# First x tiles of part two loaded and normalised earlier, and the row of ones of the stacked keys written by DMA

## The chip, the cores and the metric

The kernel runs on one core of a Trainium2 chip. The metric is the device time of one execution in microseconds; the median of three runs is given with the lowest and the highest.

## The reference

The input x is (8, 2048, 256) in float32. The reference is one transformer-like layer of two parts, each with a residual around it and layer norms without weights:

```python
x = x + layernorm(attn(layernorm(x)))
x = x + layernorm(ffn(layernorm(x)))
```

The attention is a Nystrom attention with 16 heads of size 16 and 64 landmarks, each the mean of 32 tokens:

```python
k, q, v = split_heads(x @ Wk), split_heads(x @ Wq) / 4, split_heads(x @ Wv)
q_l, k_l = means of q and of k over 32 tokens           # 64 landmarks per head
s1 = softmax(q @ k_l.T)                                 # 2048 x 64
s2 = softmax(q_l @ k_l.T)                               # 64 x 64
s3 = softmax(q_l @ k.T)                                 # 64 x 2048
out = (s1 @ (pinv(s2) @ (s3 @ v))) @ Wo + bo            # pinv: six Newton-like iterations
```

The second part mixes each token with the one before it (`xr = x_prev + mu_r * (x - x_prev)`, `xk` likewise) and computes `sigmoid(xr @ W_r.T) * (relu(xk @ W_k.T)**2 @ W_v.T)`.

## The kernel before, in words

The eight rows of the batch (2048 tokens each) go through two parts. Each engine has one program written in order; semaphores say what it waits for.

**Part one** takes the rows in two groups of four. For each row it loads x whole (`x1in`), computes mean and variance of every token (`mv1`, `rstd1`, kept for part two), pools the landmarks, projects them, stores queries and keys of the landmarks to DRAM (`lm_dram`, SyncE, line 460), and inverts s2 by six iterations of matrix products. The last inverse leaves VectorE as X (line 1028), and ScalarE's queue stores it to DRAM (`zt_dram`, line 728, semaphore `zt_out`).

**Part two** takes row by row (b) in chunks (c) of 512 tokens. Its tiles lie in the memory that part one used. The order of its stages is written out by hand: PRO once, then BODY seven times, then LAST. Every engine walks through this one list and does its share of each stage (`part2_program`). The stages at the start are: X (SyncE loads a chunk of x into `xin`, two buffers), XA (VectorE makes the normalised `xhat` of it, four instructions of 256 columns, line 1046), R (TensorE transposes xhat into the two `bank`s, ScalarE and VectorE split it into two float16 halves `xT`), AQ, AK and AV (projections), Q and K (SyncE loads the landmarks' block-diagonal tiles `q_bd` and `kA_bd`, eight transfers each), KC (SyncE stacks the halves of k into `k_stack`, twelve transfers), B1 and B2 (row maxima over q_bd and k, matmuls of line 1381, maxima of line 1086), C1 and C2 (token maxima). FS, the scores of s3, comes after all chunks of the row.

`k_stack` has 97 partitions in use: three blocks of 32 with the high and low halves of k, and in partition 96 a row of ones (KS - 1), against which `q_stack` holds the negative maxima. The ones never change; FS waits for them once.

At the joint of the parts every engine waits until part one is over. VectorE, ScalarE, SyncE and GpSimd wait for all steps and for the inverses in DRAM (`zt_out`); TensorE waits for all steps of VectorE and ScalarE, and then, in stage R, for the first xhat. Then GpSimd clears six tiles (lines 604 to 609) and writes the row of ones with four memsets on one partition (line 616), SyncE issues the first two loads of x, and VectorE makes xhat of both.

Of the kernel before, what the change touches and what calls it, by code (L numbers as in the profile page):

```python
# [15 lines left out]
def sandwich(nc, x, Wk, Wq, Wv, Wo, bo, W_r, W_k, W_v, mu_r, mu_k, out):  # L16
# [23 lines left out]
    with ctx:  # L40
        def sb(name, shape, dt=F32, c=ctx):
            return c.enter_context(nc.sbuf_tensor(name, shape, dt))

        def sem(name):
            return ctx.enter_context(nc.semaphore(name))
# [16 lines left out]
        sel4 = sb("sel4", [P, 2 * KB])  # L62
        eye = sb("eye", [P, M])
        ident16 = sb("ident16", [P, P], F16)
        eye7 = sb("eye7", [P, M], F16)
        eye15 = sb("eye15", [P, M], F16)
        eye13 = sb("eye13", [P, M], F16)
# [130 lines left out]
        def of(steps, i, *key):  # L198

            return place[id(steps)][(i, *key)]  # L200
# [53 lines left out]
        class Norm:  # L254
# [40 lines left out]
            def apply(self, dve, dst, src, g, c):  # L295
# [13 lines left out]
        bd_cleared = sem("bd_cleared")  # L309
        stack_cleared = sem("stack_cleared")  # L310
        ones_set = sem("ones_set")
        KS = 3 * 32 + 1
        x_in = [sem(f"x_in{i}") for i in range(2)]
        bank_full = [sem(f"bank{i}_full") for i in range(2)]
# [35 lines left out]

        PRO = [("X", 0), ("XA", 0), ("X", 1), ("XA", 1), ("R", 0), ("X", 2), ("X", 3), ("Q", 0), ("AK", 0), ("XA", 2),
# [79 lines left out]
        def _(sp):  # L433
            def load_rows(i, rows):
                for s in rows:
# [4 lines left out]
                    sp.dma_start(x1in[s % NX1][:, :, :], x[bass.ds(n, 1)].rearrange("a (t p) n -> p (a t) n", p=P))\  # L440
                        .then_inc(p_in[s], 16)

            load_rows(0, [0])
            for w, (dst, src) in enumerate([(wq, Wq), (wk, Wk), (wv, Wv), (wo, Wo)]):
                sp.dma_start(dst[:, :, :], src.rearrange("(k p) n -> p k n", p=P)).then_inc(weights_in, 16)
# [8 lines left out]
            for i in range(B // GR):  # L454
                load_rows(i, range(0 if i else 1, GR))
                for s in ROWS:
                    n = i * GR + s
                    sp.wait_ge(p_dve, of(dve_steps, i, "lmlo", s))
                    hold(sp)
                    sp.dma_start(lm_dram[bass.ds(n, 1)].rearrange("a p n -> p (a n)"),  # L460
                                 lm16[s][:, :, :, :].rearrange("p a k m -> p (a k m)")).then_inc(lm_out, 16)
            sp.wait_ge(lm_out, 16 * B)
            sp.wait_ge(zt_out, 16 * B)

            sp.wait_ge(p_pe, len(pe_steps))
            sp.wait_ge(p_dve, len(dve_steps))
            sp.wait_ge(p_act, len(act_steps))

            def load_q_stack(b):

# [17 lines left out]
            def stage_X(at, b, c):  # L488
                if b > 0 or c >= 2:

                    sp.wait_ge(x_applied, b * NC + c - 1)
                src = x[bass.ds(b, 1), c * CH:(c + 1) * CH, :].rearrange("a (t p) n -> p (a t) n", p=P)
                sp.dma_start(xin[c % 2][:, :, :], src).then_inc(x_in[c % 2], 16)

            def stage_Q(at, b, c):

# [65 lines left out]
        def _(pool):  # L562
# [28 lines left out]
            pool.wait_ge(const_made, 5)  # L591
            g.tensor_tensor(eye[:, :], ident[:, 0:M], ident[:, M:P], ALU.add).then_inc(const_made, 1)

            pool.wait_ge(eyes_made, 4)
            for s in ROWS:
                for t in (XT_bd, ST_bd, ZT_bd):
# [13 lines left out]
            pool.wait_ge(bd_cleared, 2)  # L610
            pool.wait_ge(stack_cleared, 1)
            pool.wait_ge(setup2, 3)
            for c in range(NC):
                if c:
                    pool.wait_ge(ones_set, c)
                g.memset(k_stack[KS - 1:KS, :, c * CH:(c + 1) * CH], 1.0).then_inc(ones_set, 1)

            def stage_OA(at, b, c):
                n = b * NC + c
# [247 lines left out]
        def _(dve):  # L867
# [162 lines left out]
                    ahead(it, 3)  # L1030


            dve.wait_ge(p_act, len(act_steps))
            dve.wait_ge(p_pe, len(pe_steps))
            dve.wait_ge(lm_out, 16 * B)
            dve.wait_ge(zt_out, 16 * B)

            def stage_XA(at, b, c):
                if b or c >= 2:

                    u = (at["R", c - 2] if c >= 2 else at["R", c + 2, 1]).bank
                    for k in range(KB):
                        dve.wait_ge(bank_full[k], u + 1)
                dve.wait_ge(x_in[c % 2], 16 * (b * 2 + c // 2 + 1))
                for t in range(NT):
                    ins = v.tensor_scalar(xhat[c % 2][:, t, :], xin[c % 2][:, t, :], mv1[b][:, c * NT + t, 0:1],
                                          rstd1[b][:, c * NT + t:c * NT + t + 1], ALU.subtract, ALU.mult)
                ins.then_inc(x_applied, 1)

            def stage_R(at, b, c):  # L1050

# [158 lines left out]
        def _(pe):  # L1210
# [209 lines left out]
            def stage_FS(at, b, i):  # L1420
                u = at["FS", i]
                if i == 0:

                    for k in range(KB):
                        pe.wait_ge(bank_drained[k], at["M", 0].bank + 1)
                    pe.wait_ge(q_stack_in, 16 * 3 * HB * (b + 1))
                    pe.wait_ge(k_stack_in, 16 * NKS * NC * (b + 1))
                    pe.wait_ge(ones_set, NC)
                    pe.wait_ge(setup2, 3)
                for w in range(2):  # L1430
                    t = 2 * i + w
                    pe.wait_ge(wide_drained[w], u.wide)
                    for a in range(PAIRS):
                        ins = mm(wide[w][:, a * P:(a + 1) * P], k_stack[0:KS, a, t * P:(t + 1) * P],  # L1434
                                 q_stack[0:KS, a, :], start=True, stop=True)
                    ins.then_inc(wide_full[w], 1)
# [195 lines left out]
```

## Time and profile before

| what | value |
|---|---|
| median of 3 runs | 1943.8 us |
| lowest, highest | 1938.8, 1947.53 us |
| the profiled execution | 1952.56 us |
| its span | 1950.8 us |
| TensorE, matmuls busy | 1590.1 us (82%) |
| VectorE busy | 1439.3 us (74%) |
| ScalarE busy | 984.0 us (50%) |
| GpSimd busy | 254.0 us (13%) |
| granted TensorE clock, mean | 0.918 |

All times of rows are microseconds from the start of the span of the profiled execution, which takes 1.8 us more in all. PE is TensorE, DVE VectorE, ACT ScalarE, POOL GpSimd, SP SyncE; a q behind a name (SPq, ACTq) is that engine's sequencer, here issuing DMAs. "L1046" is a line of the kernel. A row of a timeline merges equal instructions that follow one another. The clock is the share of full speed that TensorE was granted, 1.0 being 2.4 GHz and 0.50 being 1.2 GHz.

### The profile page before, as it was taken

The numbers are of one execution on the slowest core, as the hardware profiler recorded it, in microseconds if no ns is written. First come the engines' busy times: TensorE is split into PE (matmuls) and PEld (weight loads), VectorE is DVE, ScalarE is ACT, GpSimd is POOL, SyncE is SP. The second block draws the span as 40 slices with busy tenths as digits, with TensorE's granted clock in tenths as the row PEclk, the third lists the DMA queues.
The fourth block names the chain that finished last, engine by engine and source line by source line (L and its number), as shares of the span: only waits on it lengthen the run. The fifth ranks groups of instructions, "written<-read, shape, count | busy, mean of one in ns | idle before, by whom it ended". The sixth has DMA issues, their size and how long they took to land. (4 is left out here: it accounts for less than half of the span.)

```text
span 1950.8 us, 50437 instructions
## 1 busy us (share of the span) xinstructions
PE 1590.1 (82%) x21132; PEld 1094.9 (56%) x21132; DVE 1439.3 (74%) x3164; ACT 984.0 (50%) x1599; POOL 254.0 (13%) x134
## 2 busy tenths in 40 slices
PE   2677865786568989989988998998899899888786
PEld 1567755776335557556555744655564465556454
DVE  6889859777763796688579668957966895795465
ACT  1277714774224646545554654456465445645542
POOL 4000000001200111112011101211110121120112
PEclk9789986989778999999999999999999999999888
DMA  6400020001221212112131212213121121311110
GB/s 213 141 3 3 3 74 4 3 3 46 56 58 30 66 51 70 51 50 77 32 87 52 70 50 51 75 33 87 51 69 50 51 77 33 87 41 46 34 33 33
DMA packets 125697, 104.60 MB, mean 54 GB/s; under 512 B 30368, under 2 KB 123424, under 8 KB 125472
## 3 DMA queue, kind: packets, MB, share of 16 engines
q1 hardware_dynamic: 124320, 99.29, 18.2%
q8 instruction: 168, 2.75, 0.6%
q10 hardware_dynamic: 1152, 2.10, 0.3%
q14 instruction: 57, 0.47, 0.1%
HBM read 56.23 MB, written 19.92 MB: 39 GB/s over the span
## 5 line engine op out<-in xcount | busy, mean ns | idle before, releaser
L797 ACT ACTIVATE p<-wide 128x1024 f32<-128x1024 f32 x128 | 124.0, 1021 | 123.5 <-PE wide L1517 122.8
L1094 DVE TENSOR_REDUCE m<-wide 128x16 f16<-128x1024 f32 x128 | 150.4, 1216 | 41.8 <-PE wide L1401 41.5
L1577 PE MATMUL bank<-wrT,xrT 128*128 128x256 f32 x512 | 142.5, 440 | 46.1 <-ACT vv L763 36.1
L774 ACT ACTIVATE e<-wide 128x1024 f32<-128x1024 f32 x128 | 124.4, 1021 | 81.7 <-PE wide L1434 70.4
L1577 PEld LDWEIGHTS bank<-wrT,xrT 128*128 128x128 f32 x512 | 111.6, 223 | 72.0 <-issue 40.0
L1086 DVE TENSOR_REDUCE m<-wide 128x2 f32<-128x1024 f32 x128 | 149.8, 1212 | 2.9 <-PE wide L1381 2.9
L641 POOL TENSOR_TENSOR ob<-ob,xm 128x1024 f32<-128x1024 f32 x32 | 77.0, 2405 | 475.1 <-DVE ob L299 475.1
L1557 PE MATMUL bank<-wo,oT 128*128 128x256 f32 x512 | 120.9, 390 | 6.2 <-DVE xT L1054 3.6
L1587 PE MATMUL acc<-xkT,wkT 128*128 128x512 f32 x256 | 120.1, 613 | 7.1 <-DVE xkT L1167 7.1
L1599 PE MATMUL bank<-wvT,ka 128*128 128x256 f32 x512 | 117.6, 383 | 1.3 <-ACT x2T L822 0.8
L625 POOL TENSOR_TENSOR xm<-yy,xres 128x1024 f32<-128x1024 f32 x32 | 76.1, 2378 | 326.1 <-issue 265.7
L635 POOL TENSOR_TENSOR xkT<-x2T 128x1024 f32<-128x1024 f32 x32 | 60.6, 1893 | 433.2 <-ACT x2T L822 433.2
L1557 PEld LDWEIGHTS bank<-wo,oT 128*128 128x128 f32 x512 | 96.4, 193 | 25.7 <-issue 8.2
L1599 PEld LDWEIGHTS bank<-wvT,ka 128*128 128x128 f32 x512 | 95.3, 190 | 16.2 <-issue 1.9
L1130 DVE TENSOR_TENSOR oT<-acc,oT 128x512 f32<-128x512 f32 x64 | 42.1, 681 | 78.9 <-ACT oT L808 78.9
L1453 PE MATMUL acc<-e,vv 128*17 128x64 f32 x4096 | 77.6, 224 | 25.0 <-ACT e L774 21.0
L1343 PE MATMUL bank<-xT,w 128*128 128x512 f16 x384 | 92.0, 391 | 3.8 <-ACT x2T L822 1.9
L1343 PE MATMUL acc<-xT,w 128*128 128x512 f16 x384 | 93.3, 395 | 1.5 <-DVE xT L1054 1.5
L830 ACT ACTIVATE sg<-bank 128x512 f32<-128x512 f32 x64 | 38.1, 597 | 108.9 <-PE bank L1577 89.4
L1365 PE MATMUL bank<-w,xT 128*128 128x256 f16 x768 | 89.2, 273 | 3.8 <-ACT x2T L822 2.8
L975 DVE COPY ST_bd<-ST_d 64x1024 f16<-64x1024 f16 x192 | 81.0, 422 | 11.5 <-DVE ST_d L966 0.5
L1453 PEld LDWEIGHTS acc<-e,vv 128*17 128x17 f32 x4096 | 62.0, 99 | 42.8 <-issue 28.6
(283 smaller groups left out, 3766.9 us busy)
## 6 DMA issues: line engine op xcount, KB each, us to landing
x1in<-in_L_attn_x SPq DMA_DIRECT2D x8, 2048.0 KB, 10.0
xin<-in_L_attn_x SPq DMA_DIRECT2D x32, 512.0 KB, 4.1
k_stack<-kh SPq DMA_DIRECT2D x256, 64.0 KB, 2.0
xres<-in_L_attn_x SPq DMA_DIRECT2D x32, 512.0 KB, 4.1
out<-ob SPq DMA_DIRECT2D x32, 512.0 KB, 5.3
k_stack<-kl SPq DMA_DIRECT2D x128, 64.0 KB, 2.0
q_stack<-landmarks SPq DMA_DIRECT2D x192, 4.0 KB, 1.6
inverse<-X ACTq DMA_DIRECT2D x8, 256.0 KB, 2.2
```

The costliest lines, as they stand in the source:

```text
L774: sc.activation(e3[w][:, :], wide[w][:, :], ACT.Exp).then_inc(wide_drained[w], 1)
L797: sc.activation(p1[:, 2 * j:2 * j + 2, :], wide[w][:, :].rearrange("p (a n) -> p a n", a=2), ACT.Exp).then_inc(wide_drained[w], 1)
L975: ins = v.tensor_copy(dst[r, :, :, j * M:(j + 1) * M], src[r, :, :, :])
L1086: v.tensor_reduce(m3[:, 2 * j:2 * j + 2, c], wide[j % 2][:, :].rearrange("p (a n) -> p a n", a=2), AX.X, ALU.max).then_inc(wide_drained[j ...
L1094: v.tensor_reduce(m1[:, tiles, 2 * w:2 * w + 2, :].rearrange("p t q x -> p q t x"), wide[w][:, :].rearrange("p (q t x m) -> p q t x m", q= ...
L1343: ins = mm(dst[o][:, :], w16[:, w, wt, k, o * P:(o + 1) * P], xT[:, xt, k, :], start=(i == 0), stop=(i == len(TERMS) - 1))
L1365: ins = mm(bank[j][:, t * A:(t + 1) * A], xT[:, xt, k, tok], w16[:, 2, wt, k, :], start=(i == 0), stop=(i == len(TERMS) - 1))
L1453: ins = mm(acc[k][32 * q:32 * q + HS + 1, j * M:(j + 1) * M], vv[:, 2 * i + w, h, :], e3[w][:, h * M:(h + 1) * M], start=(w == 0 and j == ...
L1557: ins = mm(dst, oT[:, k, tok], wo[:, k, :], start=(k == 0), stop=(k == KB - 1))
L1577: ins = mm(bank[j][:, t * A:(t + 1) * A], xrT[:, k, tok], wrT[:, k, :], start=(k == 0), stop=(k == KB - 1))
L1587: ins = mm(acc[o][:, :], wkT[:, k, o * P:(o + 1) * P], xkT[:, k, :], start=(k == 0), stop=(k == KB - 1))
L1599: ins = mm(bank[j][:, t * A:(t + 1) * A], ka[:, k, tok], wvT[:, k, :], start=(k == 0), stop=(k == KB - 1))
```

## The change

Four things are done.

- SyncE issues the first two loads of x (row 0, chunks 0 and 1) right after the last landmark store of part one, behind three conditions: all rows are pooled, the last landmark projections are done, and the weights are split (`w16_lo`). These are what still reads the memory in which `xin` and `xhat` lie.
- VectorE does stage XA of the two chunks behind the last X of part one and ahead of its waits for the end of part one.
- GpSimd no longer writes the row of ones. At the start of the program it fills a tile `ones16` (128 x 128, float16), and at the joint SyncE copies it into partition 96 of `k_stack` by one DMA (32 KB), ahead of the other transfers of part two.
- The four entries X and XA of chunks 0 and 1 go from the head of PRO.

The core of the diff:

```diff
+        ones16 = sb("ones16", [P, P], F16)
...
-        PRO = [("X", 0), ("XA", 0), ("X", 1), ("XA", 1), ("R", 0), ("X", 2), ("X", 3), ("Q", 0), ("AK", 0), ("XA", 2),
+        PRO = [("R", 0), ("X", 2), ("X", 3), ("Q", 0), ("AK", 0), ("XA", 2),
...
+            def load_x(b, c):
+
+                src = x[bass.ds(b, 1), c * CH:(c + 1) * CH, :].rearrange("a (t p) n -> p (a t) n", p=P)
+                sp.dma_start(xin[c % 2][:, :, :], src).then_inc(x_in[c % 2], 16)
...
+            sp.wait_ge(p_pooled, B)
+            sp.wait_ge(p_pe, of(pe_steps, B // GR - 1, "qk", GR - 1))
+            sp.wait_ge(w16_lo, 3)
+            hold(sp)
+            load_x(0, 0)
+            load_x(0, 1)
             sp.wait_ge(lm_out, 16 * B)
             sp.wait_ge(zt_out, 16 * B)
...
+            sp.wait_ge(ones_made, 1)
+            sp.dma_start(k_stack[KS - 1:KS, :, :], ones16[:, :]).then_inc(ones_set, 16)
...
+            g.memset(ones16[:, :], 1.0).then_inc(ones_made, 1)
             pool.wait_ge(eyes_made, 4)
...
-            for c in range(NC):
-                if c:
-                    pool.wait_ge(ones_set, c)
-                g.memset(k_stack[KS - 1:KS, :, c * CH:(c + 1) * CH], 1.0).then_inc(ones_set, 1)
...
-            dve.wait_ge(p_act, len(act_steps))
-            dve.wait_ge(p_pe, len(pe_steps))
-            dve.wait_ge(lm_out, 16 * B)
-            dve.wait_ge(zt_out, 16 * B)
-
             def stage_XA(at, b, c):
...
+            for c in range(2):
+                stage_XA(None, 0, c)
+
+            dve.wait_ge(p_act, len(act_steps))
+            dve.wait_ge(p_pe, len(pe_steps))
+            dve.wait_ge(lm_out, 16 * B)
+            dve.wait_ge(zt_out, 16 * B)
...
-                    pe.wait_ge(ones_set, NC)
+                    pe.wait_ge(ones_set, 16)
```

VectorE's program at the joint, before (X is the last step of part one, xhat is stage XA, xT stage R):

```order
700 L1028 TENSOR_SCALAR X<-acc 128x512 [waits p_pe]
701 L1198 MEMSET x2T 128x2 [waits zt_out,lm_out,late_in,p_pe,p_act]
702 L1046 TENSOR_SCALAR xhat<-xin,mv,rstd 128x256 [waits x_in0]
703 L1046 TENSOR_SCALAR xhat<-xin,mv,rstd 128x256 x3
704 L1046 TENSOR_SCALAR xhat<-xin,mv,rstd 128x256 [waits x_in1]
705 L1046 TENSOR_SCALAR xhat<-xin,mv,rstd 128x256 x3
706 L1054 TENSOR_TENSOR xT<-bank,xT 128x512 [waits x_hi] x2
```

The same place after the change:

```order
700 L1040 TENSOR_SCALAR X<-acc 128x512 [waits p_pe]
701 L1053 TENSOR_SCALAR xhat<-xin,mv,rstd 128x256 [waits x_in0]
702 L1053 TENSOR_SCALAR xhat<-xin,mv,rstd 128x256 x3
703 L1053 TENSOR_SCALAR xhat<-xin,mv,rstd 128x256 [waits x_in1]
704 L1053 TENSOR_SCALAR xhat<-xin,mv,rstd 128x256 x3
705 L1213 MEMSET x2T 128x2 [waits zt_out,lm_out,late_in,p_pe,p_act]
706 L1069 TENSOR_TENSOR xT<-bank,xT 128x512 [waits x_hi] x2
```

The eight xhat instructions stand ahead of the memset that carries the waits for `zt_out`, where they stood behind it.

SyncE's queue from the last landmark stores to the loads of `q_bd`, before:

```order
15 L460 DMA landmarks<-lm 128x512 [waits p_dve] x4
16 L493 DMA xin<-in_L_attn_x 128x4x256 [waits p_dve,p_pe,p_act,zt_out,lm_out]
17 L493 DMA xin<-in_L_attn_x 128x4x256
18 L493 DMA xin<-in_L_attn_x 128x4x256 [waits x_applied] x2
19 L486 DMA q_bd<-landmarks 16x2x64 [waits bd_cleared]
```

And after the change:

```order
15 L467 DMA landmarks<-lm 128x512 [waits p_dve] x4
16 L448 DMA xin<-in_L_attn_x 128x4x256 [waits w16_lo,p_pooled,p_pe]
17 L448 DMA xin<-in_L_attn_x 128x4x256
18 L483 DMA k_stack<-ones 1x128x128 [waits p_dve,p_act,p_pe,ones_made,zt_out,lm_out]
19 L448 DMA xin<-in_L_attn_x 128x4x256 [waits x_applied] x2
20 L502 DMA q_bd<-landmarks 16x2x64 [waits bd_cleared]
```

The first two loads have left the wait for `zt_out` behind them, and the copy of the ones stands now behind that wait, ahead of chunks 2 and 3 and of `q_bd`.

## Rows read from the trace of the kernel before

**Rows 1.** Windows: stretch, length, busy (and count) per engine, clock, DMA, GB/s.
```profile
478.14:499.73 21.59, 0.00 (x0) 0.03 (x1) 15.21 (x10) 0.00 (x0) 16.76 (x10) 0.58 0.28 97
499.73:1950.80 1451.07, 1265.23 (x13200) 800.60 (x13200) 1044.38 (x2260) 728.79 (x1200) 213.59 (x96) 0.94 0.21 56
```

**Rows 2.** Timeline of TensorE: start, duration, instructions, idle time before and its releaser.
```profile
477.27 0.87 PE L1243 MATMUL acc<-ZT_d,ST_bd 128*128 128x64 f16 x24 [0.81 <-DVE ST_bd L975]
499.73 1.94 PE L1336 MATMUL bank<-ident,xhat 128*128 128x128 f32 x8 [21.59 <-DVE xhat L1046]
503.13 5.28 PE L1343 MATMUL acc<-xT,w 128*128 128x512 f16 x12 [1.46 <-DVE xT L1054]
...
511.21 0.40 PE L1381 MATMUL wide<-kh,q_bd 32*128 32x512 f16 x4
...
519.97 2.75 PE L1343 MATMUL acc<-xT,w 128*128 128x512 f16 x12
...
578.75 0.61 PE L1434 MATMUL wide<-q_stack,k_stack 97*128 97x128 f16 x8 [1.80 <-DVE m L1094]
```

**Rows 3.** Timeline of VectorE at the joint; rows may overlap, taken from several windows.
```profile
479.04 0.68 DVE L1028 TENSOR_SCALAR X<-acc 128x512 f32<-128x512 f32 x1
...
486.17 13.31 DVE L1046 TENSOR_SCALAR xhat<-xin,mv,rstd 128x256 f32<-128x256 f32 x4 [3.74 <-DMA xin<-in_L_attn_x]
...
488.60 7.28 DVE L1046 TENSOR_SCALAR xhat<-xin,mv,rstd 128x256 f32<-128x256 f32 x2
...
499.40 1.36 DVE L1046 TENSOR_SCALAR xhat<-xin,mv,rstd 128x256 f32<-128x256 f32 x4
501.57 1.46 DVE L1054 TENSOR_TENSOR xT<-bank,xT 128x512 f16<-128x512 f32 x2 [0.81 <-ACT xT L742]
```

**Rows 4.** Timeline of GpSimd at the joint; the last row is part of the one above.
```profile
482.25 0.31 POOL L604 MEMSET q_bd<- 128x256 f16 x1 [456.94 <-DMA inverse<-X]
...
484.57 0.31 POOL L609 MEMSET wbd<- 128x256 f32 x1
485.02 14.30 POOL L616 MEMSET k_stack<- 1x4096 f16 x4
...
488.59 7.14 POOL L616 MEMSET k_stack<- 1x4096 f16 x2
```

**Rows 5.** Timeline of SyncE's queue at the joint.
```profile
482.18 18.98 SPq L493 DMA_DIRECT2D xin<-in_L_attn_x  x4
501.20 3.77 SPq L486 DMA_DIRECT2D q_bd<-landmarks  x8
```

**Rows 6.** Stores of the inverses (line 728), from issue to landing.
```profile
DMA to landing us min/median/max: 2.0/2.2/3.0
```

**Rows 7.** Timeline of SyncE's queue, last landmark stores.
```profile
289.95 4.17 SPq L460 DMA_DIRECT2D landmarks<-lm  x2
```

**Rows 8.** Loads of x in part two (line 493): ns of issue min/median/max, and landing.
```profile
L493 SPq DMA_DIRECT2D xin<-in_L_attn_x x32: 368/430/593, 482.2 to 1673.2; - x32
...
DMA to landing us min/median/max: 3.9/4.1/6.2
```

**Rows 9.** Loads of k_stack from 505 us on: ns of issue, and landing.
```profile
L528 SPq DMA_DIRECT2D k_stack<-kh x256: 585/597/1583, 509.8 to 1758.9; - x128
...
DMA to landing us min/median/max: 2.0/2.0/5.1
```

**Rows 10.** The page's DMA queues: packets, MB, share of 16 engines' span.
```profile
q1 hardware_dynamic: 124320, 99.29, 18.2%
```

**Rows 11.** First loads of q_bd, 480 to 530 us, from issue to landing.
```profile
DMA to landing us min/median/max: 2.0/2.9/3.9
```

**Rows 12.** Windows around the joint, columns as in rows 1.
```profile
478.00:481.50 3.50, 0.14 (x5) 0.02 (x1) 1.72 (x3) 0.00 (x0) 0.00 (x0) 1.00 0.76 286
499.73:508.80 9.07, 7.61 (x22) 3.59 (x23) 3.11 (x7) 2.15 (x4) 0.00 (x0) 0.50 0.42 122
536.00:540.00 4.00, 3.17 (x9) 0.97 (x10) 3.65 (x4) 0.00 (x0) 0.00 (x0) 0.52 0.07 9
```

More of the change, by code:

```diff
@@ L311, in sandwich @@
         ones_set = sem("ones_set")
+        ones_made = sem("ones_made")
         KS = 3 * 32 + 1
@@ L491, in stage_X @@
                     sp.wait_ge(x_applied, b * NC + c - 1)
-                src = x[bass.ds(b, 1), c * CH:(c + 1) * CH, :].rearrange("a (t p) n -> p (a t) n", p=P)
-                sp.dma_start(xin[c % 2][:, :, :], src).then_inc(x_in[c % 2], 16)
+                load_x(b, c)
             def stage_Q(at, b, c):
```

## The prediction

> **What bounds the kernel now.** I read the windows first, because the shares of the whole span mix two programs. Part one (statistics, landmarks, inverses) and part two (attention and feed-forward) are separated by a stretch of 21.59 us in which TensorE does no matmul at all, between 478.14 and 499.73 us of the span; after it TensorE is busy 1265 of 1451 us [rows 1]. The change touches only this joint, so the question is what ends last in it, and whether anything after it runs by something else than its own chain.
>
> TensorE's own timeline gives both ends: the last product of part one at 477.27 + 0.87 = 478.14, then stage R of row 0, chunk 0 at 499.73, released by VectorE's xhat [rows 2]. VectorE's timeline shows what came before that [rows 3]: the last X of part one ends at 479.72, xhat starts at 486.17 (after a wait for the x tile) and its first four instructions take 13.31 us. GpSimd's timeline has the reason [rows 4]: four memsets of the row of ones, 3.5 us each, from 485.02 to 499.32. The second xhat starts at 488.60, just after the second memset (488.59), and the pair 488.60 to 495.88 goes in step with the pair of memsets 488.59 to 495.73: one xhat per memset. The fifth to eighth, from 499.40 on with no memset beside them, take 1.36 us together. SyncE issues the x loads only at 482.18 [rows 5], when the last inverse has landed, 2.46 us after the end of X (such a store lands 2.0 to 3.0 us after its issue, median 2.2 [rows 6]).
>
> So the 21.59 us are: 1.58 to the end of X, 2.46 until the inverses have landed, 3.99 until x has landed, 13.31 of xhat, and 0.25 from VectorE to TensorE.
>
> **The change part by part.**
>
> *Early load.* Two x loads of 512 KB go from 482.18 to behind the last landmark store on SyncE's queue, which ends at 294.12 [rows 7]; their conditions (pooling and projections of the second group done) are met by then, since those stores carry what the projections make. Behind them on that queue nothing is due until 482.18, and they land in 3.9 to 6.2 us [rows 8] with 185 us to spare. They cost nothing; the 3.99 us wait goes.
>
> *Early xhat.* VectorE does its eight xhat instructions right behind the last X, before the wait for the inverses. Four take 1.36 us: 479.72 + 1.36 = 481.08, less some 0.06 by which each starts before the one ahead has ended, 481.02, and with 0.25 of handover TensorE starts at 481.27. Eight take twice that and end at 482.4. Nobody is behind them on VectorE but the first subtraction of stage R, whose place in the old frame is 501.57, 1.84 after TensorE's start: 483.1. The new waits on SyncE and VectorE in the joint name only what was waited for before, plus a tile of ones made in the first microseconds.
>
> *The memsets.* The 14.3 us on GpSimd go; six others (482.25 to 484.88) stay. At most the last of the eight xhat touches the first of them. If every VectorE instruction were held by a memset alongside, stage R's second subtraction could start only at 484.88 instead of 483.9: 1 us at most. I take 0, since the held ones all read and write SBUF and this one reads PSUM. The Trainium skill (SBUF — State Buffer, "Who interferes with whom") calls the shared pair of VectorE and GpSimd an exclusive lock, held for a whole instruction, and says that an instruction with at most one SBUF input outside the two-port modes does not contend. The step of one xhat per memset agrees; by the rule this term is 0, by the cruder reading 1 us.
>
> *The row of ones by DMA.* No row shows a DMA of 128 pieces of 256 B into one partition. The nearest are the k_stack loads: about 0.6 us to issue, and 2.0 to 5.1 us to landing for 64 KB [rows 9]. The queue's 124320 packets took 18.2% of 16 engines' 1950.8 us [rows 10], 46 ns each; all 128 on one engine would be 5.9 us, spread over 16 engines 0.4 us. Filling the tile of ones is one more memset at the program's start, at most the 0.31 us of one with 256 columns [rows 4], on an engine that then idles for 457 us. The first reader of the ones stands at 578.75 [rows 2], 560.3 when shifted, so the landing itself costs nothing either way. What it could cost is its place ahead of the others: SyncE issues it at 482.18 (0.6 us), then x tiles 2 and 3 (0.43 each), then q_bd for 3.77 us, to 487.5. The q_bd pieces land up to 3.9 us after issue [rows 11], at 491.4. The first row maxima (L1381) ran at 511.21 [rows 2], shifted 492.7. The slack is 1.3 us, so nothing is paid; with all the ones on one engine q_bd could be the whole 5.9 us later, and 4.6 us would be paid. Between 0 and 4.6 I take 0, the side of the k_stack rows, which are the nearest. The Trainium skill (DMA: Bandwidth & Descriptors, "How many engines") takes as many of 16 engines as divide both outer dimensions, here 128 and 128, which would mean 16; no row here shows it.
>
> *The start of part two.* ScalarE still waits for the inverses, until 482.2. VectorE's first subtraction needs ScalarE's first half; it stood at 501.57 after 0.81 us of waiting for it [rows 3], shifted 483.1, which leaves ScalarE 0.9 us for one eviction. So the shift holds here too, just so; with the slowest landing of 3.0 us instead of 2.2 [rows 6] 0.8 us would be lost. The rest of the prologue follows TensorE's start.
>
> *Sum.* 499.73 - 481.27 = 18.5 us less. No wait of SyncE after the joint is on time itself; the transfers it issues are released by engines [rows 5], and the steps of part two stand in the same order. So the shift reaches the end. The profiled execution took 1952.56 us for a span of 1950.8; less 18.5 is 1934.1. It is 8.8 us above the median of the runs, 1943.8, and on that footing the forecast is 1925.3, say 1925 us. The terms taken as 0 reach from 6.4 us lost (1.0 + 4.6 + 0.8) to 2.3 us won (the clock, next).
>
> **Rivals.**
>
> *The clock stays up (1923 us).* The granted clock is 1.0 until 481.5 and 0.50, the level of 1.2 GHz, from 499.73 to 508.8 [rows 12]; it was thus still whole 3.3 us after the last matmul. Now TensorE restarts after 3.1 us, just before. If it stays at 2.4 GHz, the first K projections (12 matmuls) take 2.75 instead of 5.28 us [rows 2]: 2.5 us. But then the row maxima would be due at 490.2, and q_bd comes at 487.5 + 2.9 (median) = 490.4: 2.3 us are left. For it: the gap is shorter than the time shown. Against it: until 484.7 there are only eight transposes to do, and the window from 536 to 540 shows 0.52 with TensorE busy 3.2 of 4 us [rows 12]. The Trainium skill (TensorE: Matmul & The Clock Gate, Part 1) makes the clock follow recent activity and so allows either.
>
> *The gain is partly returned (1926 to 1934 us).* One of the losses above alone, or all of them together (6.4 us), give 1926 to 1932. For more, the prologue has to wait for transfers that no longer had 18 us of quiet: q_bd, kA_bd and the k_stack loads now queue behind one another from 482.2. The rows speak against it: that order and its distances were the same before, but for the ones.
>
> *Slower.* The mean granted clock of part two is 0.94 over 1265 us of TensorE's work [rows 1]. A rest of 18 us is gone and every later stage meets the clock's changes at another moment; if they fall worse, so that the mean is 0.926 or below, 1265 x (0.94/0.926 - 1) = 19 us eat all the gain, and from there on the kernel is slower; at 0.92 it is 1943.8 - 18.5 + 27 = 1953 us. For it: the clock does fall in part two at small pauses. Against it: the three runs of the kernel lie within 9 us of one another, and a shift of all pauses has no side.
>
> *The change does not do what it says.* If xhat were still late for another reason, TensorE would start at 486 or later, and the gain would be below 14 us (1930).
>
> **Chances.** Forecast 0.66, clock up 0.17, partly returned (with the last rival) 0.14, slower 0.03. Some 0.5% (9.7 us) is what a measurement here can tell. Faster by more: the first two whole and most of the third, 0.93; within 0.5%: 0.05; slower: 0.02. The range takes the three unslow cases with the spread of the runs (1938.8 to 1947.53, about 4 us each way): 1917 to 1933.
>
> **What would show it.** TensorE's idle stretch near 3.1 us instead of 21.6; eight xhat with about 0.4 us each right behind X; no memset of k_stack; the first K projections at either 5.3 or 2.8 us; no wait for q_bd above 1 us in front of the first L1381-type matmul; the length from stage R's start to the end of the span within 4 us of 1451. If that last length grows by 10 us or more, the forecast is wrong in its sum though right in its step.

## The result and the profile after

| | before | after |
|---|---|---|
| median | 1943.43 us (7 runs, 1936.13 to 1947.53) | 1922.87 us (7 runs, 1918.28 to 1928.98) |
| ratio | | 0.9902 (95%: 0.9878 to 0.9925) |
| profiled execution, span | 1952.56, 1950.8 | 1920.52, 1918.8 |
| granted clock, mean of the profiled execution | 0.918 | 0.932 |

The ratio with its interval comes from all the runs and is not quite the quotient of the two medians (0.9894, 20.6 us). Put on 1943.43 us it is a gain of 19.0 us, between 14.6 and 23.7. The forecast was 18.5 us and 1925 us; the result lies 2 us below it and inside the range. The two profiled executions lie 32.0 us apart, far more than the medians: that of before was 9.1 us above its median, that of the change 2.4 below. So the joint is compared below by distances inside the traces, and the whole by the ratio.

TensorE at the joint after the change, the timeline (columns as in [rows 2]):

```profile
477.15 0.87 PE L1258 MATMUL acc<-ZT_d,ST_bd 128*128 128x64 f16 x24 [0.81 <-DVE ST_bd L987]
481.28 1.94 PE L1351 MATMUL bank<-ident,xhat 128*128 128x128 f32 x8 [3.25 <-DVE xhat L1053]
484.68 5.06 PE L1358 MATMUL acc<-xT,w 128*128 128x512 f16 x12 [1.46 <-DVE xT L1069]
489.57 2.75 PE L1358 MATMUL bank<-xT,w 128*128 128x512 f16 x12
492.26 0.39 PE L1396 MATMUL wide<-kh,q_bd 32*128 32x512 f16 x4
...
559.83 0.61 PE L1449 MATMUL wide<-q_stack,k_stack 97*128 97x128 f16 x8 [1.80 <-DVE m L1109]
```

The idle stretch is 3.25 us where [rows 2] had 21.59, and stage R starts at 481.28. Here wide<-kh,q_bd (L1396) is the first row maxima and wide<-q_stack,k_stack (L1449) the first reader of the ones. VectorE, the timeline of the same place:

```profile
478.93 0.68 DVE L1040 TENSOR_SCALAR X<-acc 128x512 f32<-128x512 f32 x1
479.65 2.67 DVE L1053 TENSOR_SCALAR xhat<-xin,mv,rstd 128x256 f32<-128x256 f32 x8
482.27 0.06 DVE L1213 MEMSET x2T<- 128x2 f32 x1
483.12 1.46 DVE L1069 TENSOR_TENSOR xT<-bank,xT 128x512 f16<-128x512 f32 x2 [0.79 <-ACT xT L754]
```

All eight xhat take 2.67 us where four took 13.31 in [rows 3]. The two subtractions of stage R take 1.46 us, as in [rows 3], though GpSimd's six memsets now run beside them (next fence, GpSimd's timeline; the row of [rows 4] with k_stack has no counterpart):

```profile
482.12 0.45 POOL L620 MEMSET q_bd<- 128x256 f16 x1 [456.80 <-DMA inverse<-X]
...
484.58 0.31 POOL L625 MEMSET wbd<- 128x256 f32 x1
```

SyncE's queue, at the early loads and at the joint (the places of [rows 7] and [rows 5]), and below it the landing of the ones and of q_bd:

```profile
294.99 0.94 SPq L448 DMA_DIRECT2D xin<-in_L_attn_x  x2
```
```profile
482.05 0.59 SPq L483 DMA_DIRECT2D k_stack<-ones  x1
482.69 1.12 SPq L448 DMA_DIRECT2D xin<-in_L_attn_x  x2
483.85 3.76 SPq L502 DMA_DIRECT2D q_bd<-landmarks  x8
```
```profile
DMA to landing us min/median/max: 3.1/3.1/3.1
...
DMA to landing us min/median/max: 2.7/3.6/4.6
```

The copy of the ones takes 0.59 us to issue and 3.1 to land. q_bd lands up to 4.6 us after issue instead of 3.9 [rows 11], yet the first row maxima do not wait for it.

A second number is needed to see whether the shift travels on. I measure in each trace from the last matmul of part one (start plus duration of the row with ZT_d) to two later points: the first row maxima and the first reader of the ones, the end of the prologue. Before: 511.21 - 478.14 = 33.07 and 578.75 - 478.14 = 100.61 us [rows 2]. After: 492.26 - 478.02 = 14.24 and 559.83 - 478.02 = 81.81. So 18.83 us at the one and 18.80 at the other. At the start of stage R it is 21.59 - 3.26 = 18.33 us; the other 0.5 us come from the K projections, which took 5.06 and 2.75 us instead of 5.28 and 3.08 [rows 2], a difference of the clock.

### The profile page after: what moved, and what is told of

It reads as the page before. It is cut to its first block and busy times, and to the rows that moved or that the text cites. A ratio compares the mean times of both kernels' runs of the same rounds, so it can differ in the third digit from the quotient of the medians.

```text
span 1918.8 us, 50439 instructions
## 1 busy us (share of the span) xinstructions
PE 1579.3 (82%) x21132; PEld 1088.7 (57%) x21132; DVE 1428.2 (74%) x3164; ACT 984.5 (51%) x1599; POOL 242.3 (13%) x131
## 3 DMA queue, kind: packets, MB, share of 16 engines
q1 hardware_dynamic: 124464, 99.32, 18.5%
q8 instruction: 168, 2.75, 0.6%
## 5 line engine op out<-in xcount | busy, mean ns | idle before, releaser
L1468 PE MATMUL acc<-e,vv 128*17 128x64 f32 x4096 | 76.7, 222 | 25.8 <-ACT e L786 21.4
```

Source lines behind the costliest of these rows:

```text
L1468: ins = mm(acc[k][32 * q:32 * q + HS + 1, j * M:(j + 1) * M], vv[:, 2 * i + w, h, :], e3[w][:, h * M:(h + 1) * M], start=(w == 0 and j == ...
```

## The experiments

All runs of a group share runs of the kernel before; gains by the times are the ratio put on the median of before in that group. "Reader" is the second distance, 100.61 us in the kernel before. Each distance comes from one trace. From the row maxima to the reader it is 65.2 to 68.0 us in all traces but e1 and e6, with a mean granted clock of 0.87 in the shortest and 0.82 in the longest, and 66.25 and 67.61 us in e7 and e10, which are one kernel. So a difference of less than about 2 us at the reader can be the clock alone; the row maxima stand nearer to the joint and are the better measure there.

| run | first row maxima | reader | gain at the reader | gain by the times (95%) |
|---|---|---|---|---|
| the change | 14.24 | 81.81 | 18.8 | 19.0 (14.6 to 23.7) |
| e1 memset kept | 13.51 | 90.00 | 10.6 | 13.0 (8.6 to 17.5) |
| e2 only ones by DMA | 20.44 | 88.24 | 12.4 | 12.1 (8.0 to 16.4) |
| e3 xhat late | 17.59 | 83.65 | 17.0 | 14.6 (9.5 to 19.7) |
| e4 short memsets | 25.62 | 93.15 | 7.5 | 7.4 (3.9 to 10.9) |
| e5 clock kept | 12.19 | 77.72 | 22.9 | 22.1 (18.8 to 25.6) |
| e6 and q_bd first | 11.45 | 84.46 | 16.2 | 19.8 (16.5 to 23.3) |
| e7 chain cut | 10.11 | 76.36 | 24.3 | 24.3 (20.6 to 27.8) |
| e8 the change again | 13.71 | 81.68 | 18.9 | 21.6 (16.5 to 26.8) |
| e9 chain cut and clock | 8.44 | 73.64 | 27.0 | 27.0 (21.0 to 32.9) |
| e10 chain cut again | 10.13 | 77.74 | 22.9 | 21.4 (16.5 to 26.2) |

The medians of before in the three groups were 1947.03 (e1 to e4), 1942.15 (e5 to e8) and 1944.31 us (e9, e10), so medians of different groups are not compared.

**e1: the memsets stay on GpSimd, loads and xhat early.**

```diff
-            sp.wait_ge(ones_made, 1)
-            sp.dma_start(k_stack[KS - 1:KS, :, :], ones16[:, :]).then_inc(ones_set, 16)
...
+            for c in range(NC):
+                if c:
+                    pool.wait_ge(ones_set, c)
+                g.memset(k_stack[KS - 1:KS, :, c * CH:(c + 1) * CH], 1.0).then_inc(ones_set, 1)
```

> The changed kernel, but the row of ones is written by the four memsets of GpSimd again; loads and xhat of chunks 0 and 1 stay early. Theory (a GpSimd memset holds a VectorE instruction that reads and writes SBUF until the memset has ended, one instruction per memset): TensorE starts part two at 481.3 as in the changed kernel, but the memsets now run from about 485.0 to 499.3 beside xhat of chunk 2, which stood at 491.0 and took 1.37 us; it will end near 499.8, 7.4 us late, and ql and the row maxima behind it with it. Gain over the kernel before: 18.5 - 7.4 = 11 us. Rival (only what stands in the joint itself is held, and the early xhat is the whole gain): 18.5 us, with xhat of chunk 2 at 1.4 us.

Median 1932.88 us, ratio 0.9933 (0.991 to 0.9956). GpSimd, then VectorE, then TensorE, timelines of this run:

```profile
484.99 14.27 POOL L630 MEMSET k_stack<- 1x4096 f16 x4
```
```profile
489.64 0.69 DVE L1084 SCALAR_TENSOR_TENSOR kl<-acc,kh 128x512 f16<-128x512 f32 x1 [0.86 <-ACT kh L771]
490.25 9.48 DVE L1055 TENSOR_SCALAR xhat<-xin,mv,rstd 128x256 f32<-128x256 f32 x4
499.65 0.68 DVE L1078 SCALAR_TENSOR_TENSOR ql<-bank,qh 128x512 f16<-128x512 f32 x1
```
```profile
491.50 0.40 PE L1398 MATMUL wide<-kh,q_bd 32*128 32x512 f16 x4
500.47 1.86 PE L1382 MATMUL bank<-w,xT 128*128 128x256 f16 x8 [8.58 <-DVE ql L1078]
```

The stall moves to the next xhat, that of chunk 2: 9.48 us instead of 1.37, to 499.7, and TensorE waits 8.58 us behind the row maxima for ql. kl, which has one input in PSUM, takes its usual 0.69 us in the middle of a memset (488.56 to 492.07), so VectorE as such is not held. xhat differs from it in two things, all its tiles being in SBUF and its operation being another (TENSOR_SCALAR); no run takes these apart. The reader comes 8.2 us later than with the change; 7.4 was expected. The rival, that the early xhat is the whole gain, falls.

**e2: only the row of ones by DMA**, issued behind the first two x loads; everything else as before.

```diff
                 sp.dma_start(xin[c % 2][:, :, :], src).then_inc(x_in[c % 2], 16)
+                if b == 0 and c == 1:
+                    load_ones()
...
-            for c in range(NC):
-                if c:
-                    pool.wait_ge(ones_set, c)
-                g.memset(k_stack[KS - 1:KS, :, c * CH:(c + 1) * CH], 1.0).then_inc(ones_set, 1)
```

> The kernel before, but the row of ones comes by DMA (issued behind the first two x loads); loads and xhat stay where they were. Theory: the idle stretch of TensorE is 1.58 + 2.46 + 3.99 + 1.36 + 0.25 = 9.6 us instead of 21.6, gain 12.0 us. Rival (xhat is slow for another reason than the memsets, such as the transfers that run beside it or the first use of fresh tiles): xhat keeps 13.3 us and the gain is below 2 us.

Median 1934.77 us, ratio 0.9938 (0.9916 to 0.9959). VectorE's and TensorE's timelines:

```profile
484.98 1.38 DVE L1051 TENSOR_SCALAR xhat<-xin,mv,rstd 128x256 f32<-128x256 f32 x4 [3.79 <-DMA xin<-in_L_attn_x]
```
```profile
486.61 1.94 PE L1341 MATMUL bank<-ident,xhat 128*128 128x128 f32 x8 [9.70 <-DVE xhat L1051]
```

Idle 9.70 us, 9.6 expected, with the same transfers and fresh tiles. The memsets alone made xhat slow, and their removal is 12 of the 19 us; the early load and xhat add the other 6.4 (100.61 - 88.24 = 12.4, 88.24 - 81.81 = 6.4). The shares go by the order: without the removal, in e1, the early load and xhat are worth 10.6 us.

**e3: xhat of chunks 0 and 1 behind the wait for the inverses**, otherwise the change.

```diff
-            for c in range(2):
-                stage_XA(None, 0, c)
-
             dve.wait_ge(p_act, len(act_steps))
             ...
             dve.wait_ge(zt_out, 16 * B)
+            for c in range(2):
+                stage_XA(None, 0, c)
```

> The changed kernel, but VectorE makes xhat of chunks 0 and 1 behind the wait for the inverses in DRAM. Theory: xhat starts at 482.3 instead of 479.65, TensorE at 483.9 instead of 481.3, idle 5.8 us, 2.6 us slower than the changed kernel, gain over the kernel before 15.9 us. The memsets of the six tiles (482.1 to 484.9) now run beside xhat; by the theory of one instruction held per memset each xhat takes as long as the memset beside it, 0.3 to 0.95 us: four take about 2.1 instead of 1.4 us, so TensorE starts at 484.6. Rival (short memsets of 128 partitions hold nobody): 483.9.

Median 1932.11 us, ratio 0.9925 (0.9899 to 0.9951). VectorE, GpSimd, TensorE:

```profile
481.72 3.11 DVE L1053 TENSOR_SCALAR xhat<-xin,mv,rstd 128x256 f32<-128x256 f32 x4 [2.60 <-DMA inverse<-X]
```
```profile
482.14 1.09 POOL L622 MEMSET q_stack<- 128x1024 f16 x1
```
```profile
485.08 1.94 PE L1351 MATMUL bank<-ident,xhat 128*128 128x128 f32 x8 [7.55 <-DVE xhat L1053]
```

Short memsets over 128 partitions hold xhat as well: four take 3.11 us (I expected 2.1, the rival 1.4), and the memset of q_stack takes 1.09 instead of 0.95 us, so each side waits for the other. Idle 7.55 us is 4.3 more than with the change: 2.6 of later start and 1.7 of holding. At the reader only 1.8 us of it are left (83.65 against 81.81, where 3.3 were expected): the K projections took 4.11 us here and 5.06 in the change, and the stretch from the row maxima to the reader 66.06 us at a mean clock of 0.84 against 67.57 at 0.82. The place of xhat ahead of `zt_out` is worth more than the wait alone, since it also leaves the memsets behind.

**e4: sixteen memsets of 1024 elements**, otherwise the kernel before.

```diff
-            for c in range(NC):
+            for c in range(4 * NC):
...
-                g.memset(k_stack[KS - 1:KS, :, c * CH:(c + 1) * CH], 1.0).then_inc(ones_set, 1)
+                g.memset(k_stack[KS - 1:KS, :, c * P:(c + 1) * P], 1.0).then_inc(ones_set, 1)
```

> The kernel before, but the row of ones is written by sixteen memsets of 1024 elements instead of four of 4096. Theory (one xhat is held per memset, for the rest of that memset): a memset takes about 3.53 / 4 = 0.9 us, so each xhat takes about 0.95 us, the first four end at 486.2 + 3.8 = 490.0, TensorE starts at 490.2, gain 9.5 us, and the eight xhat are through by 494. Rival (VectorE shares the ports with GpSimd at a fixed ratio as long as memsets run): xhat keeps its 3.6 us, TensorE starts near 499.7, gain 0.

Median 1938.09 us, ratio 0.9962 (0.9944 to 0.998). GpSimd, VectorE, TensorE:

```profile
486.05 16.28 POOL L616 MEMSET k_stack<- 1x1024 f16 x16
```
```profile
487.21 8.22 DVE L1046 TENSOR_SCALAR xhat<-xin,mv,rstd 128x256 f32<-128x256 f32 x8 [3.75 <-DMA xin<-in_L_attn_x]
```
```profile
491.52 1.94 PE L1336 MATMUL bank<-ident,xhat 128*128 128x128 f32 x8 [12.34 <-DVE xhat L1046]
496.72 5.28 PE L1343 MATMUL acc<-xT,w 128*128 128x512 f16 x12 [3.26 <-DVE xT L1054]
```

GpSimd writes for longer than before (16.28 us), yet xhat takes 1.03 us each (8.22 / 8) instead of 3.6: the price of one xhat is one memset (16.28 / 16 = 1.02), not a share of the port. The idle stretch is 12.34 us, 12.1 expected. All eight are held now, so the subtractions behind them come late and TensorE waits 3.26 us for them, 1.8 more than before [rows 2]; this I had left out, and it makes 7.5 us of the expected 9.5.

**e5: TensorE kept busy in the joint.** The change, with matmuls that nobody reads.

```diff
-            pe.wait_ge(p_dve, len(dve_steps))
...
+            def warm(count):
+                for _ in range(count):
+                    mm(wide[0][:, 0:512], ident16[:, :], w16[:, 0, 0, :, :].rearrange("p k n -> p (k n)"),
+                       start=True, stop=True)
+
+            pe.wait_ge(p_dve, of(dve_steps, B // GR - 1, "ZTlo", ITERS - 1, 1))
+            warm(12)
+            pe.wait_ge(p_dve, len(dve_steps))
...
                     ins.then_inc(bank_full[k], 1)
+                if n == 0:
+                    warm(6)
```

> The changed kernel with 12 matmuls of 512 columns without use in front of stage R of chunk 0 and 6 behind it, which write a bank that nobody reads before it is overwritten. They keep TensorE busy through the joint. Theory (the clock rival of the prediction): the granted clock stays 1.0, the eight transposes take 1.3 instead of 1.9 us and the first K projections 2.75 instead of 5.1, but q_bd lands only 3.6 to 4.6 us after its last issue at 487.2, so the first row maxima start at 490.8 to 491.8 instead of 492.3: 0.5 to 1.5 us gained, and a wait for q_bd in front of them on TensorE. Rival (q_bd has slack enough): row maxima at 489.8, 2.5 us gained. Second rival (the clock falls anyway): nothing gained.

Median 1919.05 us, ratio 0.9886 (0.9868 to 0.9903). TensorE's timeline and the window from 477.13 to 489.50:

```profile
483.30 2.75 PE L1366 MATMUL acc<-xT,w 128*128 128x512 f16 x12 [0.71 <-DVE xT L1069]
485.89 2.75 PE L1366 MATMUL bank<-xT,w 128*128 128x512 f16 x12
489.32 0.40 PE L1404 MATMUL wide<-kh,q_bd 32*128 32x512 f16 x4 [0.67 <-DMA q_bd<-landmarks]
```
```profile
477.13:489.50 12.37, 10.45 (x54) 4.92 (x54) 9.02 (x22) 3.47 (x6) 2.76 (x6) 1.00 0.56 176
```

The clock stays at 1.00 and the K projections take 2.75 us; a wait of 0.67 us for q_bd appears, as foretold. At the row maxima 2.05 us come in against the first trace of the change and 1.5 against its second (e8, 13.71), where 0.5 to 1.5 were expected; at the reader it is 4.1. The windows from the row maxima to the reader, of the change and of this run, say where the other 2 us are:

```profile
492.26:559.83 67.57, 46.72 (x353) 25.96 (x353) 49.71 (x58) 15.92 (x27) 0.00 (x0) 0.82 0.28 65
```
```profile
489.32:554.85 65.53, 45.26 (x352) 25.09 (x353) 48.92 (x56) 15.09 (x26) 0.00 (x0) 0.84 0.28 62
```

TensorE's matmuls took 1.46 us less at a slightly higher clock, and the wait of 0.48 us for ql behind the row maxima is gone, having passed beside the wait for q_bd. The clock's part lies behind the joint and within the spread between traces of one kernel, so it is no effect of the extra matmuls that this run could show.

**e6: the same, and q_bd ahead of x chunks 2 and 3 and of the ones.**

```diff
-        PRO = [("R", 0), ("X", 2), ("X", 3), ("Q", 0), ("AK", 0), ("XA", 2),
+        PRO = [("R", 0), ("Q", 0), ("X", 2), ("X", 3), ("AK", 0), ("XA", 2),
...
-            sp.wait_ge(ones_made, 1)
-            sp.dma_start(k_stack[KS - 1:KS, :, :], ones16[:, :]).then_inc(ones_set, 16)
...
+                if b == 0 and c == 3:
+                    sp.wait_ge(ones_made, 1)
+                    sp.dma_start(k_stack[KS - 1:KS, :, :], ones16[:, :]).then_inc(ones_set, 16)
```

> As the one before (matmuls without use in the joint), and SyncE issues q_bd ahead of x chunks 2 and 3 and of the ones. Theory: q_bd is issued from 482.9 to 486.7 and lands by 489.6, so the first row maxima start at 489.8 counted as in the changed kernel, 14.24 - 2.5 = 11.8 us after the last matmul of part one. Rival (nothing but the clock bounded them): same as the run before.

Median 1923.05 us, ratio 0.9898 (0.988 to 0.9915). TensorE and VectorE:

```profile
489.69 0.40 PE L1404 MATMUL wide<-kh,q_bd 32*128 32x512 f16 x4
492.99 4.09 PE L1388 MATMUL bank<-w,xT 128*128 128x256 f16 x24 [2.91 <-DVE ql L1076]
```
```profile
490.86 1.38 DVE L1053 TENSOR_SCALAR xhat<-xin,mv,rstd 128x256 f32<-128x256 f32 x4 [2.34 <-DMA xin<-in_L_attn_x]
```

The row maxima come 11.45 us after part one (11.8 expected), the wait for q_bd is gone, and in its place xhat of chunk 2 waits 2.34 us for its x tile and TensorE 2.91 us for what stands behind it. V projections then run slower (4.09 instead of 2.78 us), and the reader is 2.7 us later than with the change and 6.7 later than in e5. Of the stretch from the row maxima to the reader, 7.5 us longer than in e5 (73.01 against 65.53), 4.5 are matmuls that took longer at a mean clock of 0.79 (49.74 against 45.26 us busy) and the rest is waiting. A transfer moved forward in one queue moved another back onto the chain. The times do not show the loss: the interval for the gain, 16.5 to 23.3 us, holds the change's 18.8 and not quite this trace's 16.2.

**e7: the chain cut.** The edits on the change are told in the expectation; besides them the copy of the ones goes behind x chunk 3. The main lines:

```diff
+                    if i == B // GR - 1 and it == ITERS - 2:
+                        for c in range(2):
+                            stage_XA(None, 0, c)
...
+            sp.wait_ge(bd_cleared, 2)
+            load_bd(q_bd, False, 0, 0, q_bd_in)
+            load_bd(kA_bd, False, 1, 0, kA_bd_in)
...
-            pe.wait_ge(p_dve, len(dve_steps))
+            pe.wait_ge(p_dve, of(dve_steps, B // GR - 1, "ZTlo", ITERS - 1, 0))
...
+                if b == 0 and c == 0:
...
+                    act.wait_ge(zt_out, 16 * B)
```

> A version meant to be faster than both. xhat of chunks 0 and 1 is made in an idle stretch of VectorE in the fifth iteration of the last inverse; q_bd and kA_bd lie in memory free since the pooling and are loaded at about 300 us; the last four inverses are stored by SyncE's queue; ScalarE waits for them only in front of the first V eviction, VectorE only in front of the first row maxima, TensorE starts stage R when bank 0 is free. Theory: stage R starts 0.2 us after the last matmul, the K projections 3.3 us after it (VectorE's subtractions stand behind its last X), at full clock, the row maxima 8.7 us after it instead of 14.2: 5.5 us less than the changed kernel. Rival: the early xhat delays the inverse by up to its own 2.7 us, or the first row maxima wait for the inverses in DRAM, and 1 to 3 us are left.

Median 1916.84 us, ratio 0.9875 (0.9857 to 0.9894). TensorE's timeline:

```profile
479.12 1.06 PE L1361 MATMUL bank<-ident,xhat 128*128 128x128 f32 x8
482.48 4.33 PE L1368 MATMUL acc<-xT,w 128*128 128x512 f16 x12 [2.29 <-DVE xT L1076]
```

and VectorE's, with the early xhat inside the inverse:

```profile
442.03 0.86 DVE L1010 COPY ST_bd<-ST_d 64x1024 f16<-64x1024 f16 x2
442.92 2.67 DVE L939 TENSOR_SCALAR xhat<-xin,mv,rstd 128x256 f32<-128x256 f32 x8
447.08 0.69 DVE L1001 SCALAR_TENSOR_TENSOR ST_d<-bank,ST_d 128x512 f16<-128x512 f32 x1 [1.49 <-ACT ST_d L719]
```

The traces show no cost of the early xhat to the inverse: the next step starts 5.05 us after the copies, and 5.06 in e8, where VectorE is idle for 4.21 us instead. Stage R follows part one without a gap. The forecast of 5.5 us was for the row maxima, and there 4.1 us came (10.11 against 14.24): the K projections took 4.33 us instead of the 2.75 of full clock. The windows of the pause and of the projections show when the clock fell:

```profile
480.18:482.48 2.30, 0.01 (x2) 0.04 (x2) 1.92 (x4) 0.75 (x2) 0.00 (x0) 0.96 1.02 383
482.48:486.65 4.17, 4.17 (x13) 1.52 (x14) 0.69 (x1) 0.60 (x1) 2.12 (x4) 0.61 0.61 163
```

In the pause of 2.29 us the mean is 0.96, so the clock fell at its very end; in the second trace of this kernel (e10) it is 1.00 in the pause and 0.60 in the projections. The reader is 5.4 us earlier than with the change in this trace and 4.1 in e10 (77.74 against 81.81), so its nearness to 5.5 is luck.

**e8: the change again.**

> The changed kernel once more, beside the others of this group. Theory: 18.8 us less than the kernel before by the times (ratio 0.990), with the first row maxima 14.2 us after the last matmul of part one as in its first trace; what the span after them takes says how much of a difference between two traces is the spread of part two (1439.6 us in the trace of before, 1426.5 in the first trace of the change). Rival: part two itself is shorter by the change, then it is near 1427 again.

Median 1918.93 us, ratio 0.9889 (0.9862 to 0.9915). TensorE's timeline, and windows of the pause and of the transposes behind it:

```profile
482.20 1.29 PE L1351 MATMUL bank<-ident,xhat 128*128 128x128 f32 x8 [3.25 <-DVE xhat L1053]
485.11 5.02 PE L1358 MATMUL acc<-xT,w 128*128 128x512 f16 x12 [1.63 <-DVE xT L1069]
```
```profile
478.94:482.20 3.26, 0.01 (x2) 0.03 (x1) 3.23 (x9) 0.00 (x0) 0.00 (x0) 1.00 0.78 295
482.20:482.80 0.60, 0.60 (x6) 0.60 (x7) 0.60 (x3) 0.00 (x0) 0.00 (x0) 1.00 0.39 143
482.80:483.50 0.70, 0.69 (x5) 0.28 (x3) 0.45 (x3) 0.41 (x1) 0.47 (x2) 0.57 0.00 0
```

The pause is the same 3.25 us, but here the clock is whole to its end and through the first transposes, and falls while the others run; the K projections still take 5.02 us. The row maxima stand at 13.71 us, 0.5 earlier than in the first trace. From the row maxima to the end it has 1419.7 us, where the rival named 1427. From the reader to the end the trace has 1912.3 - 560.62 = 1351.7 us, the first trace of the change 1359.0 and that of before 1372.1. The same kernel thus differs by 7 us between two traces in a part that the change does not touch, and the trace of before was 9.1 us above its own median, so 13 us between before and after there are no evidence of a gain. Both ratios of the change hold 18.8 us in their intervals.

**e9 and e10: the cut chain with ten matmuls without use behind stage R, and the cut chain again.**

```diff
                     ins.then_inc(bank_full[k], 1)
+                if n == 0:
+                    for _ in range(10):
+                        mm(wide[0][:, 0:512], ident16[:, :], w16[:, 0, 0, :, :].rearrange("p k n -> p (k n)"),
+                           start=True, stop=True)
```

> The version with the cut chain plus ten matmuls without use of 512 columns (2.1 us) between stage R and the K projections of chunk 0. Theory (in the version with the cut chain the clock still fell in this pause: its K projections took 4.33 us): they take 2.75 us, the first row maxima stand 8.6 us after the last matmul of part one instead of 10.1, the first reader of the ones 74.8 instead of 76.4. By the times 1.6 us less, which the spread of the runs hides. Rival (another wait follows, such as the row maxima on VectorE waiting for the inverses in DRAM): below 0.5 us at the first reader.

> The version with the cut chain once more, on the same chip as the one beside it. Theory: first reader of the ones 76.4 us after the last matmul of part one, as before, and 24 us less than the kernel before by the times (ratio 0.9875). Rival (the first measurement was a lucky one): ratio above 0.989, as the change has it.

e9: median 1917.08 us, ratio 0.9861 (0.9831 to 0.9892). e10: 1922.53 us, 0.989 (0.9865 to 0.9915). TensorE in e9:

```profile
482.31 2.75 PE L1373 MATMUL acc<-xT,w 128*128 128x512 f16 x12
...
487.58 0.39 PE L1413 MATMUL wide<-kh,q_bd 32*128 32x512 f16 x4
```

e9: row maxima 8.44 us after part one (8.6 expected), reader 73.64 (74.8 expected), the shortest of all. Behind the row maxima TensorE now waits 1.25 us for ql, 0.47 in e7, since on VectorE the xhat of chunk 2 ahead of ql waits 0.68 us for its x tile; and yet the stretch from there to the reader is shorter (65.20 us at a mean clock of 0.87, 66.25 in e7 at 0.85): the surplus over the expected is the clock. By the times e9 beats the kernel before clearly, and the change by less than the runs can separate (0.9861 against 0.9902 and 0.9889, intervals overlapping). e10: row maxima 10.13 us, as in e7, reader 77.74 where 76.4 was expected, and the ratio is the 0.989 that the rival named; its interval holds both 0.9875 and the change's 0.9889, so the times do not decide. That the cut chain is faster than the change is shown by its traces (row maxima 10.11 and 10.13 against 14.24 and 13.71, reader 76.4 and 77.7 against 81.8 and 81.7), not by its times.

## Why the prediction was right

- *What bounded the joint.* Right, and shown: e1 and e4 move and shrink the stall with the memsets, and e2, which takes away only them, leaves the 9.7 us of the other terms (9.6 by the prediction's sum).
- *Early xhat.* Right: TensorE's start was put 3.13 us after the last matmul (481.27) and came 3.26 after it (481.28, part one having ended 0.12 us earlier in this trace).
- *The remaining memsets, taken as 0 of at most 1 us.* Right: the subtractions keep their 1.46 us, and kl in e1 its 0.69 us beside a memset. The Trainium skill's rule (SBUF — State Buffer, "Who interferes with whom") agrees with this and with e4's one xhat per memset. What e3 adds is that xhat, had it stood behind the wait, would have paid 1.7 us for them.
- *The ones by DMA, 0 of at most 4.6 us.* Right: 3.1 us to landing, no wait behind it; 5.9 us on a single engine did not happen, though no row says how many engines took part. The slack of q_bd, put at 1.3 us, was real but thin: e5 is ready for the row maxima 2.7 us earlier than the first trace of the change, waits 0.67 us and starts them 2.05 earlier. Its q_bd was issued as long after the last matmul as in the change (5.82 and 5.83 us), so some 2.05 us is the slack in that trace, and 1.5 in the second.
- *The clock rival.* It did not come: the K projections took 5.06 us (the forecast case had 5.28). The windows of the pause and of what follows it, mean 0.67 and 0.50:

```profile
478.02:481.28 3.26, 0.01 (x1) 0.03 (x1) 3.23 (x9) 0.00 (x0) 0.00 (x0) 0.67 0.78 295
481.28:489.20 7.92, 6.46 (x19) 3.14 (x20) 3.12 (x8) 1.79 (x3) 2.77 (x6) 0.50 0.53 152
```

  In the trace of before the clock was whole until 481.5 [rows 12]; here it fell within the 3.26 us of the pause. I had read the one fall as if it had to come that late. In e8 it did come later, the rival's condition was met, and still only 0.5 us was won at the row maxima (13.71 against 14.24), with the K projections at 5.02 us: the eight transposes and the pause of 1.63 us behind them did not hold the clock, which is what the prediction had put against the rival. e5 shows that the size was fair: at the row maxima 2.05 and 1.5 us, by the two traces of the change, against the 2.3 foretold.
- *The shift reaches the end.* 18.83 us at the row maxima, 18.80 at the reader. From there to the end it is argued and not shown by a trace, since the traces spread by more there; the 19.0 us by the times agree. One sign that the prediction named did not hold: from stage R's start to the end of the span the change took 1918.8 - 481.28 = 1437.5 us, 13.6 less than the 1451.07 of [rows 1], and e8 1430.1, where 4 us either way were allowed. That is no gain of the change in part two as far as is known: the trace of before was 9.1 us above its median and that of the change 2.4 below, and the times of all runs leave hardly more than the joint explains. The 2 us between 1925 and 1922.87 are within that spread; no step is known that explains them.
- *The range.* By its own words, from 1923 less 4 to 1932 more 4, it would be 1919 to 1936 and not 1917 to 1933. The measured 1922.87 us lies in both.
- *Slower by a worse clock in part two.* The mean from the row maxima to the end is 0.95 after and 0.94 before; in e1 to e10 the gain by the times agrees with that at the reader within its interval (e6 misses it by 0.3 us, on the side of more gain).

## What to carry to other kernels

When VectorE slows down tenfold for some instructions, look at GpSimd's row at the same time: here each xhat, an instruction of 0.4 us from SBUF to SBUF, lasted as long as the memset beside it, even though that wrote one partition only. Long writes to one partition belong to a DMA or to a place where VectorE does instructions like kl, which has an input in PSUM and was not held. Move what the first stage of a new part needs into the part before, and after each such move ask which transfer of the queue is needed next: the slack of q_bd was 1.5 to 2 us, and putting it first made x late. A gain under 1% is best followed as a distance between two events in the trace, close behind the place of the change; the times of the same kernel spread over 5 to 18 us, and even the distance over 67 us of work by 1.4 us between two traces of one kernel.

## What was not expected of the hardware

- GpSimd's memset of 1024 float16 elements takes 0.95 us on one partition (the shortest of the sixteen in e4) and 0.95 us on 128 partitions (q_stack in the kernel before, with nothing beside it): the number of partitions did not count. With 4096 elements on one partition it takes 3.5 us.
- After TensorE's last matmul the clock was whole for 3.4 us in the trace of before and fell after about 1.1 us in that of the change (0.67 over 3.26 us is 1.1 us at 1.0 and the rest at 0.50). In e8, the same kernel with the same pause, it fell about 4 us after that matmul, while the transposes ran. In e7 and e10 it was lost at the end of a pause of 2.2 to 2.3 us or as the projections behind it began. Which pause costs the clock cannot be read from its length; the matmuls of e5 and e9 that filled the pauses kept it each time.
- Both engines can be held: in e3 the memset of q_stack beside xhat took 1.09 us, alone 0.95.
